# A four-layer Mamba stack and an FP4 FFN on one core: main loop written out, input normalisation and weight quantisation moved into the Mamba prologue, TensorE's side work laid anew on the 16 slots of a turn

## The chip, the core and the metric

One Trainium2 chip, one of its cores. The metric is the device time of one execution in microseconds (us), median of several runs. Engines: PE (TensorE, matmuls), DVE (VectorE), ACT (ScalarE), POOL (GpSimd) and SP (SyncE, which here only issues DMAs).

## What is computed

With `x` of 4 x 2048 x 256 in fp32 (8192 tokens, model width 256, inner width 512, 16 states, convolution of 4 taps, rank 16):

```
x = x + mamba_stack(layernorm(x));  x = x + fp4_ffn(layernorm(x))
mamba_stack, 4 layers:
  xs, z = split(x @ in_w.T);  xc = silu(conv4(xs) + conv_b)
  dt, B, C = split(xc @ xp_w.T);  delta = softplus(dt @ dt_w.T + dt_b)
  h[t] = exp(delta[t] * A) * h[t-1] + delta[t] * xc[t] * B[t]     (512 channels x 16 states)
  y = (sum over states of h * C + xc * D_skip) * silu(z) @ out_w.T
  x = layernorm(y + x) * ln_w + ln_b
fp4_ffn:  q = blockwise FP4 quantise and dequantise, blocks of 16
  down(q(silu(q(x) @ q(wg).T) * (q(x) @ q(wu).T))) with q(wd)
```

## The kernel before, in words

Three blocks of code run one after the other, and the engines meet between them. `normalise_input` brings the 16 chunks of 512 tokens through SBUF two at a time, normalises them on DVE and ACT and writes them to the DRAM buffer `xbuf`. `mamba_layers` runs 64 turns (4 layers x 16 chunks). `fp4_ffn` first quantises and transposes its weights (three pieces of `wgu`, two of `wd`), then runs 16 chunks.

A turn `g` of `mamba_layers` has 16 slots `s`, one for each (32 channels x 4) x (4 states) group: four tiles of 128 rows x 512 tokens. In program order, each engine does in slot `s`:

- DVE: `scan(s,0)`, in slots 2, 6, 10, 14 a `gate` (multiplies the summed states `acc` by `silu(z)`), `times_b(s,1)`, `scan(s,1)`, `scan(s,2)`, `times_b(s+1,0)`, `scan(s,3)`. `times_b` is L935 (`bu<-durep,B_all`, half a slot's tiles), `scan` is L950. LayerNorm statistics of the turn before come in slot 8, their moments in slot 9.
- PE: `broadcast_b(s+1)` (L455, fills the single PSUM tile `B_all`; it waits for `times_b(s,1)`, which reads the old one), then `sum_states(s-2)` (L473, sums `hc` into `acc`), then the slot's side work for the next chunks: `convolve` (L503) in slots 0, 13, 14, 15, `project_x` (L510) in 2, `project_dt` in 3 and 4, `project_out` (L531) in 5 and 6, `project_in` of z in 8 and 9 (L493), `transpose_x` (L483) in 10, `project_in` of xs in 11 and 12. The skip term (L462) opens a quarter of four slots: it comes before `sum_states` in slots 2, 6, 10, 14. All of these but the first two share two PSUM tiles, `W[0]` and `W[1]`, which ACT must have read before PE fills them again.
- ACT: `keep_states(s-1)` (L612, waits for the last scan of the slot before), `exp(s+1)` (L603, 4 tiles), then the copies out of `W`: `copy_z` (L706) of z0, z1 in slot 9 and z2, z3 in 10, `root_guess` and `copy_xT` in 11, `copy_xs` in 12 and 13, `normalise` in 14.
- POOL: `times_c(s)` (L832, `hc<-h,crep`, two instructions), and whole-chunk work: `silu_xc` (L837) ahead of `times_c(2)`, `softplus` steps in slots 7, 8, 10, 11, `variance` (L858) in 10, `affine` (L879 and L883) at the end of slot 15. `project_x` on PE waits for `silu_xc`.
- SP: all loads and stores in one order; `x_res` has one buffer, so `store_x` waits for `affine`, and the next `load_res` for that store.

The first two and the last two turns are written out (`turns`); the 60 between are a loop of 15 iterations of four turns, with register arithmetic for counts and addresses. Nothing but this hand-written order and the semaphores sets what runs when.

Of the kernel before, what the change touches and what calls it, by code (L numbers as in the profile page):

```python
# [5 lines left out]
F32 = mybir.dt.float32  # L6
# [5 lines left out]
P = 128  # L12
T = 512
# [6 lines left out]

LN2 = 0.6931471805599453
# [32 lines left out]
def normalise_input(nc, x, xbuf, CH, sem, x_stored):  # L54

    xv = x.rearrange("(c t p) d -> c p t d", t=NT, p=P)
    ov = xbuf.rearrange("(c t p) d -> c p t d", t=NT, p=P)
    D = x.shape[1]
    with ExitStack() as ctx:
        def sb(name, shape):  # L60
            return ctx.enter_context(nc.sbuf_tensor(name, shape, F32))

        xt = sb("n0_x", [P, 2, NT, D])
        st = sb("n0_stats", [P, NT, 6])
        mean, diff = sb("n0_mean", [P, 2, NT]), sb("n0_diff", [P, NT])
        ve, lnv, guess = sb("n0_var", [P, 2, NT]), sb("n0_ln", [P, 2, NT]), sb("n0_guess", [P, 2, NT])
        tmp, root = sb("n0_tmp", [P, NT]), sb("n0_root", [P, NT])
        loaded = [sem("n0_loaded0"), sem("n0_loaded1")]
        stats, means, var_ready, ln_done, guess_ready = (sem("n0_" + s) for s in ("stats", "means", "var", "ln", "guess"))
        newton, root_done, normed = sem("n0_newton"), sem("n0_root"), sem("n0_normed")  # L70
        block = ctx.enter_context(nc.Block())

        @block.sync
        def _(sp):
            sp.dma_start(xt[:, 0], xv[0]).then_inc(loaded[0], 16)
            sp.dma_start(xt[:, 1], xv[1]).then_inc(loaded[1], 16)
            with sp.Fori(0, CH // 2) as i:
                for b in range(2):
                    sp.wait_ge(normed, 2 * i + b + 1)
                    sp.dma_start(ov[2 * i + b], xt[:, b]).then_inc(x_stored, 16)  # L80
                    sp.wait_ge(x_stored, 16 * (2 * i + b) + 16)

                    sp.dma_start(xt[:, b], xv[(2 * i + 2 + b) % CH]).then_inc(loaded[b], 16)
            for b in range(2):
                sp.wait_ge(loaded[b], 16 * (CH // 2 + 1))

        @block.scalar
        def _(act):
            act.preload_act_table_set(EXP_LN)
            with act.Fori(0, CH // 2) as i:  # L90
                for b in range(2):
                    act.wait_ge(var_ready, 2 * i + b + 1)
                    act.activation(lnv[:, b], ve[:, b], ACT.Ln).then_inc(ln_done, 1)
                    act.wait_ge(ln_done, 2 * i + b + 1)
                    act.activation(guess[:, b], lnv[:, b], ACT.Exp, scale=-0.5).then_inc(guess_ready, 1)

        @block.vector
        def _(dve):
            with dve.Fori(0, CH // 2) as i:
                for b in range(2):  # L100
                    c = 2 * i + b
                    dve.wait_ge(loaded[b], 16 * i + 16)
                    for t in range(NT):
                        dve.bn_stats(st[:, t], xt[:, b, t]).then_inc(stats, 1)
                    dve.wait_ge(stats, NT * c + NT)
                    mean_variance(dve, means, 6 * c, st, D, mean[:, b], diff[:], ve[:, b], var_ready)
                    dve.wait_ge(guess_ready, c + 1)
                    newton_root(dve, newton, 3 * c, ve[:, b], guess[:, b], tmp[:], root[:], root_done)
                    dve.wait_ge(root_done, c + 1)
                    for t in range(NT):  # L110
                        ins = dve.tensor_scalar(xt[:, b, t], xt[:, b, t], mean[:, b, t:t + 1], root[:, t:t + 1],
                                                ALU.subtract, ALU.mult)
                    ins.then_inc(normed, 1)


def mamba_layers(nc, xbuf, w, NL, L, sem, x_stored):
# [13 lines left out]
    assert KD == 2 and DB == 4 and CS == 4 and TOT % 4 == 0 and TOT >= 12 and CH % 4 == 0 and CH >= 4  # L130

    xv = xbuf.rearrange("(c t p) d -> c p t d", t=NT, p=P)

    with ExitStack() as ctx:
# [37 lines left out]
        hc = sb("hc", [P, 8, T])  # L172
        carry = sb("carry", [P, NA])
# [32 lines left out]
        set_up = sem("set_up")  # L206
# [78 lines left out]
        def _(sp):  # L285
# [5 lines left out]
            def load_x(n):  # L291
                c = ready(n % CH)
                if positive(n):
                    sp.wait_ge(w_filled[1], fill(1, n - 1, "tr") + 1)
                if isinstance(n, int):
                    sp.wait_ge(x_stored, 16 * (min(n, CH) + 1))
                sp.dma_start(x_in[:], xv[c]).then_inc(x_loaded, 16)
# [1389 lines left out]
```

## Time and profile before

| what | value |
|---|---|
| median of 3 runs (lowest, highest) | 8526.1 us (8520.08, 8530.0) |
| profiled execution, own time | 8524.19 us |
| its span, first to last instruction | 8522.4 us |
| busy, DVE / POOL / PE / ACT | 93% / 82% / 76% / 63% |
| mean granted clock of TensorE | 0.90 |

A row of the page or of a view names the line, the engine, the operation and the tiles (written `<-` read), a count `x`, and times. "Idle before" is the time the engine stood still just before these instructions, and the arrow names what ended it. A window view gives, for each stretch, each engine's busy time and the granted clock of TensorE as a share of full speed.

### The profile page before, as it was taken

Reading aid. Unit: us, or ns where it says so; the run is one execution under the profiler, and the core shown is the slowest. Engines: PE = TensorE matmul, PEld = TensorE weight load, DVE = VectorE, ACT = ScalarE, POOL = GpSimd, SP = SyncE. Lnnn points to the kernel's source line nnn. Section 1 sums busy time; section 2 is a strip of 40 time slices with the busy share of each in tenths; the row PEclk is TensorE's granted clock in tenths of the full one; section 3 lists DMA queues with packets and bytes.
Section 4 is the critical chain, followed back from the end, with each engine's and each line's share of the span. In section 5 each row is a group of like instructions: output and inputs, shape, how many; then the busy total and the mean of one; then the engine's idle time right before and its main releaser. Section 6 shows DMA issues by size and latency. Waiting matters only on the chain. (4 is left out here: it accounts for less than half of the span.)

```text
span 8522.4 us, 96647 instructions
## 1 busy us (share of the span) xinstructions
PE 6497.0 (76%) x21028; PEld 2513.0 (29%) x21028; DVE 7936.9 (93%) x8028; ACT 5407.2 (63%) x8725; POOL 6990.0 (82%) x3390
## 2 busy tenths in 40 slices
PE   3778777777777777877778777777777777764888
PEld 1222222222222222222222222222222222221555
DVE  3999999999999999999999999999999999995777
ACT  2666666666676666667666666666666666752444
POOL 1888888888888898888888888988888888884555
PEclk9899998988998899889899898989898988986999
DMA  4455443445444544445444454544554444541110
GB/s 134 98 117 120 116 115 97 114 119 132 112 104 111 121 115 113 107 117 123 118 114 112 101 118 115 121 117 107 117 119 117 112 106 106 124 112 43 37 38 30
DMA packets 567641, 909.46 MB, mean 107 GB/s; under 512 B 58288, under 2 KB 202032, under 8 KB 565936
## 3 DMA queue, kind: packets, MB, share of 16 engines
q1 hardware_dynamic: 566960, 902.24, 44.1%
q8 instruction: 201, 3.29, 0.2%
q14 instruction: 480, 3.93, 0.2%
HBM read 715.36 MB, written 186.65 MB: 106 GB/s over the span
## 5 line engine op out<-in xcount | busy, mean ns | idle before, releaser
L832 POOL TENSOR_TENSOR hc<-h,crep 128x1024 f32<-128x1024 f32 x2048 | 4785.2, 2361 | 837.0 <-PE acc L473 755.7
L950 DVE TENSOR_TENSOR_SCAN h<-dA,carry,bu 128x512 f32<-128x512 f32 x3072 | 3769.8, 1266 | 94.3 <-issue 51.8
L935 DVE TENSOR_TENSOR bu<-durep,B_all 128x1024 f32<-128x1024 f32 x2048 | 2485.6, 1214 | 192.1 <-DMA durep<-du_dram 142.5
L603 ACT ACTIVATE dA<-drep,cur 128x512 f32<-128x512 f32 x4096 | 2618.7, 710 | 13.9 <-DMA drep<-delta_dram 13.8
L455 PE MATMUL B_all<-dtc,spread_b 128*128 128x512 f32 x2048 | 1352.2, 747 | 1646.5 <-DVE bu L935 1645.0
L612 ACT COPY carry<-h 128x4 f32<-128x4 f32 x1023 | 201.0, 197 | 2232.2 <-DVE h L950 2184.8
L473 PE MATMUL acc<-hc,gather 128*32 128x512 f32 x8192 | 1279.9, 701 | 4.4 <-POOL hc L832 4.4
L950 DVE TENSOR_TENSOR_SCAN h<-dA,bu 128x512 f32<-128x512 f32 x1024 | 1197.0, 1206 | 9.0 <-ACT dA L603 8.9
L493 PE MATMUL work<-xT,inw 128*128 128x512 f32 x2048 | 1020.2, 643 | 59.5 <-ACT xT L623 48.9
L455 PEld LDWEIGHTS B_all<-dtc,spread_b 128*128 128x128 f32 x2048 | 366.8, 212 | 2330.2 <-DVE bu L935 2266.2
L503 PE MATMUL work<-xs,taps 128*128 128x512 f32 x2048 | 965.2, 614 | 0.0
L493 PEld LDWEIGHTS work<-xT,inw 128*128 128x128 f32 x2048 | 400.6, 207 | 756.1 <-issue 652.1
L503 PEld LDWEIGHTS work<-xs,taps 128*128 128x128 f32 x2048 | 376.6, 194 | 617.6 <-issue 617.6
L531 PE MATMUL work<-outw,sz 128*128 128x256 f32 x2048 | 490.5, 383 | 0.0
L473 PEld LDWEIGHTS acc<-hc,gather 128*32 128x32 f32 x8192 | 173.0, 116 | 972.3 <-issue 686.1
L844 POOL TENSOR_TENSOR quad<-quad,xs 128x2048 f32<-128x2048 f32 x64 | 289.4, 4523 | 154.2 <-ACT quad L701 154.2
L531 PEld LDWEIGHTS work<-outw,sz 128*128 128x128 f32 x2048 | 395.6, 193 | 55.9
L837 POOL TENSOR_TENSOR xc<-xc,quad 128x2048 f32<-128x2048 f32 x64 | 290.0, 4531 | 144.8 <-ACT quad L668 144.8
L1258 PE MATMUL f_gu<-f_wguT,f_xqT 128*128 128x512 f32 (+1 forms) x768 | 341.7, 598 | 72.8 <-ACT f_xqT L1345 65.9
L462 PE MATMUL acc<-xc,skip 128*128 128x512 f32 x512 | 337.6, 749 | 0.0
L854 POOL TENSOR_TENSOR relu<-za,xc 128x2048 f32<-128x2048 f32 x64 | 290.5, 4539 | 0.1
L850 POOL TENSOR_TENSOR za<-quad,relu 128x2048 f32<-128x2048 f32 x64 | 290.0, 4531 | 0.1
(166 smaller groups left out, 6683.6 us busy)
## 6 DMA issues: line engine op xcount, KB each, us to landing
drep<-delta_dram SPq DMA_DIRECT2D x1024, 256.0 KB, 6.0
durep<-du_dram SPq DMA_DIRECT2D x1024, 256.0 KB, 6.7
crep<-c_dram SPq DMA_DIRECT2D x1024, 64.0 KB, 6.4
delta_dram<-za SPq DMA_DIRECT2D x64, 1024.0 KB, 4.3
du_dram<-relu SPq DMA_DIRECT2D x64, 1024.0 KB, 5.3
x_in<-xbuf SPq DMA_DIRECT2D x65, 512.0 KB, 3.9
x_res<-xbuf SPq DMA_DIRECT2D x64, 512.0 KB, 3.9
xbuf<-x_res SPq DMA_DIRECT2D x64, 512.0 KB, 5.6
```

The lines of the kernel that those rows point to most:

```text
L455: pe.matmul(B_all[:], spread_b[:, s % QS, :], dtc[:, p_, :], start=True, stop=True).then_inc(bb_ready, 1)
L462: pe.matmul(acc[:], skip[:, q, :], xc[:, p_, q, :], start=True, stop=False, skip_group_check=True)
L473: ins = pe.matmul(acc[32 * k:32 * k + 32, :], gather[:], hc[:, 4 * (s % 2) + k, :], start=False, stop=s % QS == QS - 1, skip_group_check=True)
L493: ins = pe.matmul(W[b][:], inw[:, k, z * DI + e * P:z * DI + (e + 1) * P], xT[:, k, :], start=k == 0, stop=k == KD - 1)
L503: ins = pe.matmul(W[b][:], taps[:, 4 * e + k, :], xs[:, e, k:k + T], start=k == 0, stop=k == 3)
L531: ins = pe.matmul(half, sz[:, p_, k, t * P:(t + 1) * P], outw[:, k, :], start=False, stop=k == DB - 1)
L603: act.activation(dA[:, 4 * (s % 2) + k, :], drep[q % 2][:, k, :], ACT.Exp, scale=cur[:, p_, 4 * s + k:4 * s + k + 1]).then_inc(da_ready, 1)
L832: pool.tensor_tensor(hc[:, pair, :], h[:, pair, :], crep[:, j:j + 1, :].to_broadcast([P, 2, T]), ALU.mult).then_inc(hc_ready, 1)
L854: pool.tensor_tensor(relu[:], za[:], xc[:, p_], ALU.mult).then_inc(du_ready, 1)
L935: dve.tensor_tensor(bu[:, 2 * k:2 * k + 2, :], durep[q % 2][:, 2 * k:2 * k + 2, :], B_all[:].unsqueeze(1).to_broadcast([P, 2, T]), ALU.mul ...
L950: dve.tensor_tensor_scan(h[:, r, :], dA[:, r, :], bu[:, k, :], start, ALU.mult, ALU.add).then_inc(scanned, 1)
L1258: ins = pe.matmul(gu[:, at:at + width], xqT[:, t % 2, k, :], wguT[:, k, at:at + width], start=k == 0, stop=k == KD - 1)
```

## The change

- `normalise_input` is gone. The 16 raw chunks are loaded, at the start of `mamba_layers`, into tiles that the turns use later (`h`, `hc`, `dA`, `durep`), in batches of 1, 3, 4, 4, 4 chunks; DVE and ACT normalise a batch at a time while PE, ACT and POOL already work on chunk 0.
- The FFN's weights are quantised on DVE and transposed in the same prologue (`quantise_piece`, `turn_piece`, `copy_piece`), saved to DRAM, and only loaded at the start of `fp4_ffn`.
- `turns` writes out all 64 turns; every count and address is then a constant.
- PE: `project_out` works by 128 tokens, one in slots 5 and 6, two in 7; z0, z1 in slot 8, z2 in 9, z3 in 10, ahead of the transposes; the skip term follows `sum_states` of the group's member 1, 0, 0 or 2 (`SKIP_AT`), and the first `sum_states` of a quarter starts the accumulation. The taps of `convolve` run newest first.
- ACT: `copy_out` in slots 7 and 8, `copy_z` of z2 in 10 and z3 in 11, `root_guess` in 12, `normalise` in 15.
- POOL: `variance` in 11, `newton_step` in 13, `affine` after `times_c(0)` of the next turn. DVE: statistics in 9, moments in 10.

```diff
@@ turns
-            turn(0, 0)
-            turn(1, 1)
-            with eng.Fori(0, (TOT - 4) // 4) as i:
-                for r in range(2, 6):
-                    turn(4 * i + r, r % 4)
-            turn(TOT - 2, 2)
-            turn(TOT - 1, 3)
+            for g in range(TOT):
+                turn(g, g % 4)
@@ prologue, sync
+            load_raw(0)
             (the five constants)
             load_inw(0, 0)
+            load_raw(1)
             load_mid(0)
+            load_raw(2)
             load_skip(0, 0)
+            load_raw(3)
+            load_raw(4)
+            store_normed(0)
+            store_normed(1)
+            sp.wait_ge(n0_stored[0], 16)
+            sp.wait_ge(n0_stored[1], 48)
             load_x(1)
+            for i in range(3):
+                load_piece(i)
+            store_normed(2)
             store_c(0, 0)
...
+            for i in range(3, PIECES):
+                load_piece(i)
             store_delta(0, 0)
...
+            sp.wait_ge(piece_copied, PIECES)
+            sp.dma_start(wguT_dram, wguT).then_inc(weights_saved, 16)
@@ sum_states
-                if s % QS == 0:
-                    skip_term(n, p_, s // QS)
+                q = s // QS
+                if s % QS == 0 and positive(DB * n + q):
+                    pe.wait_ge(acc_read, DB * n + q)
...
+                if s % QS == SKIP_AT[q]:
+                    skip_term(n, p_, q)
@@ prologue, tensor
+            turn_piece(0)
             transpose_x(1)
+            turn_piece(1)
             for e in range(DB):
                 project_in(1, e, 0)
+            turn_piece(2)
@@ turn, tensor
-                        if s in (5, 6):
+                        if s in (5, 6, 7):
                             project_out(g - 1, other, s - 5)
+                        if s == 7:
+                            project_out(g - 1, other, 3)
                     if not is_last(g):
-                        if s in (8, 9):
-                            project_in(nxt, 2 * (s - 8), 1)
-                            project_in(nxt, 2 * (s - 8) + 1, 1)
+                        if s == 8:
+                            project_in(nxt, 0, 1)
+                            project_in(nxt, 1, 1)
+                        if s in (9, 10):
+                            project_in(nxt, s - 7, 1)
@@ turn, scalar
-                        if s in (9, 10):
-                            copy_z(n, other, 2 * (s - 9))
-                            copy_z(n, other, 2 * (s - 9) + 1)
+                        if s == 9:
+                            copy_z(n, other, 0)
+                            copy_z(n, other, 1)
+                        if s == 10:
+                            copy_z(n, other, 2)
+                        if s == 11:
+                            copy_z(n, other, 3)
-                        if s == 11:
+                        if s == 12:
                             root_guess(g - 1)
@@ turn, gpsimd
+            pool.wait_ge(weights_saved, 48)
-                        if s == 10:
+                        if s == 11:
                             variance(g - 1)
-                    if not is_first(g):
-                        if s == 15:
-                            affine(g - 1, 0)
-                            affine(g - 1, 1)
+                    if s == 0 and isinstance(g, int) and g >= 2:
+                        affine(g - 2, 0)
+                        affine(g - 2, 1)
@@ prologue, vector: quantise_piece (waits and increments between the steps left out)
+                dve.tensor_reduce(fp_max[:, 0:nb], blocks, AX_X, ALU.max, apply_absolute_value=True)
+                dve.tensor_scalar(fp_scale[:, 0:nb], fp_max[:, 0:nb], 1.0 / 6.0, 1e-12, ALU.mult, ALU.max)
+                dve.tensor_scalar(fp_nudged[:, 0:nb], fp_scale[:, 0:nb], 1.0 + 2.0 ** -21, None, ALU.mult)
+                dve.reciprocal(fp_rec[:, 0:nb], fp_nudged[:, 0:nb])
+                dve.tensor_tensor(blocks, blocks, spread(fp_rec), ALU.mult)
+                dve.tensor_scalar(ex.bitcast(U32), v.bitcast(U32), 0x7F800000, None, ALU.bitwise_and)
+                dve.tensor_scalar(ex, ex, 1.0, MAGIC, ALU.max, ALU.mult)
+                dve.tensor_tensor(v, v, ex, ALU.add)
+                dve.tensor_tensor(v, v, ex, ALU.subtract)
+                dve.tensor_tensor(blocks, blocks, spread(fp_scale), ALU.mult)
@@ prologue, vector
+            n0_statistics(0)
+            n0_normalise(0)
             work_out_a()
+            n0_statistics(1)
+            for i in range(2, len(BATCHES)):
+                n0_statistics(i)
+                n0_normalise(i - 1)
+            n0_normalise(len(BATCHES) - 1)
+            for i in range(PIECES):
+                quantise_piece(i)
             times_b(group(0, 0), 0)
+            dve.wait_ge(piece_turned, PIECES)
+            dve.wait_ge(piece_copied, PIECES)
@@ fp4_ffn, sync
-            sp.dma_start(wgu_in[:].rearrange("p g (t d) -> p (g t) d", d=D),
-                         w["wgu"].rearrange("t p d -> p t d")).then_inc(S["wgu_loaded"], 16)
-            sp.dma_start(wd_in[:], w["wd"].rearrange("(t p) i -> p t i", p=P)).then_inc(S["wd_loaded"], 16)
             load(0, 0)
+            sp.dma_start(wguT[:], wguT_dram).then_inc(S["wgu_loaded"], 16)
+            sp.dma_start(wdT[:, 0:GT - 1], wdT_dram[:, 0:GT - 1]).then_inc(S["wd_loaded"], 16)
```

In `fp4_ffn` the loops over the weight pieces on PE, ACT, POOL and DVE are gone and the counts shifted by as much.

## Rows read from the trace of the kernel before

**Rows 1.** The page's first part: busy time, share of the span, instructions of each engine.

```profile
PE 6497.0 (76%) x21028; PEld 2513.0 (29%) x21028; DVE 7936.9 (93%) x8028; ACT 5407.2 (63%) x8725; POOL 6990.0 (82%) x3390
```

**Rows 2.** Window view, the 64 turns (first scan to end of last): busy times, granted clock.

```profile
216.00:7744.20 7528.20, 5825.52 (x18754) 2126.89 (x18754) 7334.60 (x6902) 5026.88 (x8062) 6560.23 (x2990) 0.90 0.48 113
```

**Rows 3.** Waits of DVE in the turns: us in total, times, longest us.

```profile
DVE h L950 <- issue: 51.8, 8, 6.7
DVE bu L935 <- PE B_all L455: 46.2, 78, 1.3
DVE h L950 <- ACT dA L603: 44.6, 21, 6.5
DVE bu L935 <- DMA durep<-du_dram: 40.8, 35, 2.3
```

**Rows 4.** Groups of instructions, DVE in the turns: busy, mean ns, idle before, its releasers.

```profile
L950 DVE TENSOR_TENSOR_SCAN h<-dA,carry,bu 128x512 f32<-128x512 f32 x3072 | 3769.8, 1266 | 94.3 <-issue 51.8 <-ACT dA L603 35.8 <-POOL hc L832 6.7
...
L950 DVE TENSOR_TENSOR_SCAN h<-dA,bu 128x512 f32<-128x512 f32 x1024 | 1197.0, 1206 | 9.0 <-ACT dA L603 8.9
```

**Rows 5.** Timeline of DVE: first scan of turn 6; start, length, idle before.

```profile
919.16 1.28 DVE L950 TENSOR_TENSOR_SCAN h<-dA,carry,bu 128x512 f32<-128x512 f32 x1 [6.25 <-issue]
```

**Rows 6.** Timeline of DVE and PE ahead of the turns.

```profile
4.41 1.41 DVE L104 BATCH_NORM_STATS2 n_stats<-n_x 128x6 f32<-128x256 f32 x4 [4.41 <-DMA n_x<-in_x]
8.01 1.38 DVE L111 TENSOR_SCALAR n_x<-n_x,n_mean,n_root 128x256 f32<-128x256 f32 x4
...
112.89 1.94 PE L483 MATMUL work<-ident,x_in 128*128 128x128 f32 x8 [112.89 <-DMA x_in<-xbuf]
...
214.69 1.23 DVE L935 TENSOR_TENSOR bu<-durep,B_all 128x1024 f32<-128x1024 f32 x1 [101.69 <-DMA durep<-du_dram]
```

**Rows 7.** Timeline of DVE and POOL at the start of the FFN.

```profile
7793.29 1.22 DVE L1061 TENSOR_REDUCE f_f_qa_amax<-f_wgu_in 128x64 f32<-128x1024 f32 x1 [7.05 <-DMA f_wgu_in<-in_wgu]
...
7840.27 2.35 POOL L1417 TENSOR_TENSOR f_xa<-f_xa,f_xm 128x1024 f32<-128x1024 f32 x1
```

**Rows 8.** Timeline of POOL at the head of turn 20, which starts at 2567.5.

```profile
2570.05 2.36 POOL L879 TENSOR_TENSOR x_res<-x_res,lnw 128x1024 f32<-128x1024 f32 x1
...
2574.79 9.32 POOL L832 TENSOR_TENSOR hc<-h,crep 128x1024 f32<-128x1024 f32 x4
...
2584.08 4.52 POOL L837 TENSOR_TENSOR xc<-xc,quad 128x2048 f32<-128x2048 f32 x1
```

**Rows 9.** Timeline of POOL at the head of turn 1 (no affine), which starts at 329.7.

```profile
334.42 4.76 POOL L832 TENSOR_TENSOR hc<-h,crep 128x1024 f32<-128x1024 f32 x2 [1.75 <-DVE h L950]
341.37 4.75 POOL L832 TENSOR_TENSOR hc<-h,crep 128x1024 f32<-128x1024 f32 x2 [2.19 <-DVE h L950]
```

**Rows 10.** Timeline of PE and DVE in slots 2 and 3 of turn 20.

```profile
2583.87 2.08 PE L455 MATMUL B_all<-dtc,spread_b 128*128 128x512 f32 x2 [5.18 <-DVE bu L935]
...
2589.25 3.70 PE L510 MATMUL work<-xc,xpw 128*128 128x512 f32 x8
...
2592.79 1.02 PE L455 MATMUL B_all<-dtc,spread_b 128*128 128x512 f32 x2
...
2593.94 1.23 DVE L935 TENSOR_TENSOR bu<-durep,B_all 128x1024 f32<-128x1024 f32 x1 [1.05 <-PE B_all L455]
```

**Rows 11.** Window view, PE's work between the two in slot 2: the last columns are clock and DMA.

```profile
2583.90:2589.20 5.30, 5.30 (x12) 1.35 (x12) 5.27 (x5) 5.27 (x10) 4.70 (x2) 0.52 0.01 3
```

**Rows 12.** DMA issues of the page: out<-in, count, KB each, median us to landing.

```profile
xbuf<-x_res SPq DMA_DIRECT2D x64, 512.0 KB, 5.6
```

**Rows 13.** Timeline of all engines in slots 10 and 11 of turn 31 (slot 11 starts at 3945.2).

```profile
3945.26 1.09 PE L483 MATMUL work<-ident,x_in 128*128 128x128 f32 x8
...
3945.43 2.56 ACT L603 ACTIVATE dA<-drep,cur 128x512 f32<-128x512 f32 x4
...
3947.65 1.12 PE L455 MATMUL B_all<-dtc,spread_b 128*128 128x512 f32 x2 [1.29 <-DVE bu L935]
...
3949.86 1.21 DVE L935 TENSOR_TENSOR bu<-durep,B_all 128x1024 f32<-128x1024 f32 x1
```

More of the change, by code:

```diff
@@ L19 @@
 SIGMOID = "sigmoid_and_others"
+MAGIC = 1.5 * 2.0 ** 22
+EXP_CENTRE = -(1.0 - 3e-6)
 LN2 = 0.6931471805599453
@@ L51, in mean_variance @@
     dve.tensor_tensor(ve, ve, diff, ALU.add).then_inc(done, 1)
[L54 to L113, printed above, removed]
@@ L129, in mamba_layers @@
     C_DB, C_CB = 0, DB
-    assert KD == 2 and DB == 4 and CS == 4 and TOT % 4 == 0 and TOT >= 12 and CH % 4 == 0 and CH >= 4
+    SKIP_AT = (1, 0, 0, 2)
     xv = xbuf.rearrange("(c t p) d -> c p t d", t=NT, p=P)
+    raw = x.rearrange("(c t p) d -> c p t d", t=NT, p=P)
+    GP, IN = w["wgu"].shape[0] // NT, w["wd"].shape[1]
+    GT, PIECES = -(-IN // P), GP + w["wd"].shape[0] // P
+    assert KD == 2 and DB == 4 and CS == 4 and TOT % 4 == 0 and TOT >= 12 and CH == 16 and PIECES <= 5 and KD * GP * T <= 8 * T and GT * D <= DB * T
+    BATCHES = [(0, 1), (1, 4)] + [(c, c + 4) for c in range(4, CH, 4)]
     with ExitStack() as ctx:
@@ L501, in convolve @@
                 wait_free(pe, b, fill(b, n, f"c{e}"))
-                for k in range(4):
-                    ins = pe.matmul(W[b][:], taps[:, 4 * e + k, :], xs[:, e, k:k + T], start=k == 0, stop=k == 3)
+                for k in (3, 2, 1, 0):
+                    ins = pe.matmul(W[b][:], taps[:, 4 * e + k, :], xs[:, e, k:k + T], start=k == 3, stop=k == 0)
                 ins.then_inc(w_filled[b], 1)
@@ L525, in project_out, with turn_piece @@
                     pe.wait_ge(res_loaded, 16 * (m + 1))
[L526 to L532 removed]
+                if t % 2 == 0:
+                    wait_free(pe, j, out_fill(j, m))
+                half = W[j][:, (t % 2) * D:(t % 2 + 1) * D]
+                pe.matmul(half, ident[:], x_res[:, t, :], start=True, stop=False)
+                for k in range(DB):
+                    ins = pe.matmul(half, sz[:, p_, k, t * P:(t + 1) * P], outw[:, k, :], start=False, stop=k == DB - 1)
+                if t % 2 == 1:
+                    ins.then_inc(w_filled[j], 1)
+            def turn_piece(i):
+                pe.wait_ge(piece_ready, i + 1)
+                if i > 0:
+                    pe.wait_ge(piece_copied, i)
+                if i < GP:
+                    for k in range(KD):
+                        for t in range(NT):
+                            ins = pe.transpose(bu[:, 2 + k, t * P:(t + 1) * P],
+                                               piece[i % 3][:, t * D + k * P:t * D + (k + 1) * P], ident[:])
+                else:
+                    for k in range(GT):
+                        rows = min(P, IN - k * P)
+                        ins = pe.transpose(bu[0:rows, 2 + k // 4, (k % 4) * P:(k % 4 + 1) * P],
+                                           piece[i % 3][:, k * P:k * P + rows], ident[:])
+                ins.then_inc(piece_turned, 1)
             pe.wait_ge(consts, 80)
@@ L550, in _ @@
             broadcast_b(group(0, 0), 0)
+            for i in range(3, PIECES):
+                turn_piece(i)
             def turn(g, ph):
@@ L584, in _ @@
                 sum_states(group(TOT - 1, s), 1)
-            for j in range(2):
-                project_out(TOT - 1, 1, j)
+            for t in range(NT):
+                project_out(TOT - 1, 1, t)
         @block.scalar
@@ L737, in _ @@
             keep_halo(0)
+            n0_guess_root(1)
             for e in range(DB):
                 copy_conv(0, 0, e)
+            n0_guess_root(2)
             tanh_xc(0, 0)
             act.preload_act_table_set(EXP_LN)
+            for i in range(3, len(BATCHES)):
+                n0_guess_root(i)
             copy_proj(0, 0)
@@ L753, in _ @@
             keep_halo(1)
+            copy_piece(2)
             for e in range(2):
                 copy_conv(1, 1, e)
+            act.wait_ge(n0_stored[3], 64)
             exp(group(0, 0), 0)
+            for i in range(3, PIECES):
+                copy_piece(i)
             def turn(g, ph):
@@ L1011, in turn @@
                     times_b(nxt, 0)
-                    if s == 9 and not is_first(g):
+                    if s == 10 and not is_first(g):
                         dve.wait_ge(stats, g)
@@ L1109, in fp4_ffn @@
     KD = D // P
-    GP = w["wgu"].shape[0] // NT
-    DP, IN = w["wd"].shape[0] // P, w["wd"].shape[1]
+    IN = w["wd"].shape[1]
     GT = -(-IN // P)
```

305 lines of the change are left out of this document (184 added, 121 removed).

## The prediction

> **What bounds the kernel now.** I read the page's busy shares first: DVE is at 93%, well above POOL and PE [rows 1]. Then the window of the 64 turns: DVE is busy 7334.6 of 7528.2 us there [rows 2], 97%. So the turns are DVE's own work plus about 194 us in which it waits; a change in another engine's order counts only through what it adds to or takes from these waits. DVE's waits say which they are [rows 3]: 51.8 us with nothing shown, 44.6 for `exp`, 46.2 for `B_all` from PE, 40.8 for the replicated `du`. The first is eight waits of up to 6.7 us, each ahead of the first scan of a turn, as in turn 6 [rows 5]; six of the waits on `exp` are as long and stand in the same place (the group of carried scans has 35.8 us of them [rows 4]). That is 51.8 + 35.8 = 87.6 us in 14 waits of 6.3 on average, and the loop of 15 iterations jumps back 14 times. What is left to PE and DMA is small and spread. Outside the turns lie 216 us before the first scan and the FFN after.
>
> **The change, part by part.** The sum is made against the profiled execution: span 8522.4 us, own time 8524.2, 1.9 below the median of the runs, 8526.1.
>
> *Prologue.* Before, the first batch is normalised from 4.41 to 9.4 [rows 6], but chunk 0 reaches PE only at 112.89 and the first `times_b` runs at 214.69: a chain of 101.8 us after 112.9 us that are all input normalisation and the start of the block. After, chunk 0 goes to PE straight from the normalised tile at about 13 us (my estimate: the 9.4, and then the steps that work out `A`, for which ACT waits). The chain itself stays: 13 + 101.8 = 115, so 99.7 us are saved if nothing delays it. What DVE adds beside it: 16 chunks at 1.41 + 1.38, 45 us, and five times the 2.2 us of small steps between the two, 11; five pieces of six full-width steps of up to 1.22 us [rows 7] and four small ones, about 9 us for each of the three wide ones and 6.5 for the two narrow ones, 40. 4.4 + 45 + 11 + 40 and 4 for `A` make 104, under 115 if the loads keep up. PE's `turn_piece(1)` and `(2)` stand ahead of chunk 1's convolution, and SP's `load_piece(4)`, ahead of `store_delta`, waits for piece 1 to be turned; a few us late on DVE go straight into the chain. POOL then waits until the weights are saved, a few us that its lead over DVE's second slot mostly covers. I take 90 saved, with 75 and 99 as the ends.
>
> *FFN start.* POOL's first addition, at 7840.27, moves to where the first load lands, about when DVE now gets its first weights, 7793 less 1 us [rows 7]: 48 us saved. The load of the finished weights lies beside the normalising and quantising of chunk 0.
>
> *Loop written out.* The 14 waits of 6.3 us go: 88 saved. The turns 0 to 5 run without one, with the same instructions in a row, so straight code is fed in time, and nothing in the trace speaks against that. The ends are 0 and 88. The Trainium skill (Runtime: NRT & Kernel Launch, Instruction fetch mechanics) says that a taken branch whose target is out of the fetched window stalls the engine and that kernels therefore prefer full unrolling; by it too these 88 us go, and the trace has the 6.25 us it does not state.
>
> *Skip term after the sum, `copy_out` later.* POOL's `times_c` waits for PE's sum; with the skip's two matmuls, of a broadcast's shape (1.02 or 2.08 us [rows 10]), behind the sum, POOL reaches `softplus` and `du` earlier. Of the 40.8 us of `du` waits, and the small ones on `exp` (44.6 - 35.8 = 8.8), I take 33 as saved; 0 and 50 are the ends. The PE rearrangement also evens out slots 5 to 7, so that the 46.2 us of `B_all` waits, taken as a whole, are struck out and new ones counted from nothing below.
>
> *`affine` after `times_c(0)`: the wait in slot 3.* `project_x` waits for `silu_xc`, and PE runs `broadcast_b(4)` behind it, which DVE needs between its third and fourth scan of slot 3. In turn 20 POOL runs `affine` at once after `times_c(15)`, from 2.55 us into the turn, then both `times_c`, and `silu_xc` from 16.58 to 21.1 [rows 8]. POOL would otherwise idle there: without `affine`, `times_c(0)` can't start before 4.72 and ends at 9.48, as in turn 1 [rows 9], because it waits for PE's sum and for the scans. With the new order: 9.48, `affine` 4.78, `times_c(1)` 4.68, `silu_xc` 4.52 make 23.5, which is 2.4 us later. From the start of `project_x` (3.70 us) over the broadcast (1.02) to `times_b(4,0)` it takes 4.69 us, and I give `project_x` 0.15 to start [rows 10]: 28.3. DVE on its own would be there at 25.4 (turn 20 starts a sequence: 2593.94 less its wait of 1.05 and less 2567.5), and in the other turns 12 carried scans of 0.06 us more later [rows 4], at 26.1. POOL, paced by DVE's shorter slots in turns like 20, ends at 23.2 there. So the wait is 2.2 us, and 0.45 more in turns that start a sequence. That is the floor.
>
> On top comes the clock. PE idled 5.18 us before the broadcast in slot 2, which then took 2.08 us where the later one took 1.02 [rows 10], and in the 5.3 us that follow the granted clock is 0.52, the lower level of 1.2 GHz mostly [rows 11]; broadcast, skip and sum fill that stretch, and `project_x` starts at the full clock. After the change the skip is gone from slot 2: the broadcast starts at 16.4 into the turn as now, it and the sum, both at the low clock, end at about 20.4, PE stands about 3.2 us until 23.6, and `project_x` comes out of the pause. I put half of the chain of 4.72 us at the lower level, 2.4 us more; the ends are 0 and 4.7. The Trainium skill (TensorE: Matmul & The Clock Gate, The HAM clock gate) says the array's default state is throttled and that activity releases it; it speaks for the extra, and without it the sum would be 61 x 2.4 = 146 us lower. So 61 turns at 2.2 + 2.4, and 0.45 more in 15 of them: 288 us added. Everything later in the turn shifts along with DVE, so none is won back. On SP `store_x` waits for the later `affine` (its end moves from 7.3 to 14.3 us into the turn), and `load_res`, `load_delta` and `load_du` queue behind it: 14.3 + 5.6 for the store [rows 12] and as much again at most for the load is 25.5 us, before `project_out` in slot 5 at 35, and the `load_delta` behind it waits for slot 3's `exp` in any case. No cost.
>
> *z3 in slot 10: the wait in slot 11.* `transpose_x` fills `W[1]`, which holds z3 until ACT has copied it, and ACT now does so in slot 11 after `exp`: 3945.43 + 2.56, and 0.6 for the copy, make 3948.6. Half the transposes (0.55) and the broadcast (1.12 and 0.13) follow: 3950.4, against 3949.86 on DVE [rows 13]. The floor is 0.55 us. Slot 9 now has one projection in place of two (eight matmuls like those of `project_x`, 3.70 us), so PE's pause before slot 10 grows by 1.85 us, and skip, z3 and transposes run partly at the low clock; I take 1.0 us for 62 turns, 62 us (34 to 124). `root_guess` now stands ahead of `copy_xs` in slot 12 and waits for a `variance` that POOL does behind `times_c(11)`; `project_in` of xs2 waits behind that with no room to spare: 20 us (0 to 60).
>
> Sum: -90 - 48 - 88 - 33 - 46 + 288 + 62 + 20 = +65. 8524.2 + 65 = 8589 us.
>
> **The rivals.** *The clock is no part of it.* PE's work in slot 2 raises the clock as now and the pause is too short to lower it. For it: `project_x` runs at full clock now in turn 20. Against: it does so only because 5.3 us of work precede it. It would give floors only, 288 - 146 + 34 + 10: 8589 - 146 - 28 - 10 = 8405, faster. This is the case on the other side: it is decided by whether `project_x` takes nearer 3.7 or 7.4 us, and the sign changes where the clock costs 1.3 us a turn instead of 2.4.
>
> *No wait in slot 3 at all.* `silu_xc` isn't what PE is late for, because POOL makes up the 2.4 us. Against: between `times_c(1)` and `silu_xc` nothing in its order leaves room. 8405 - 142 = 8263.
>
> *The long waits stay.* The written-out code is fetched no faster, or the 14 waits are not the jump's. Against: their place and number. 8589 + 88 = 8677.
>
> *The whole chain at the low clock.* 4.7 instead of 2.4 us in 61 turns: 8589 + 140 = 8729, more if slot 11 goes the same way.
>
> **How the numbers follow.** Forecast 0.44 (its own range 8500 to 8660), no clock 0.30, no wait in slot 3 0.07, waits stay 0.06, whole chain low 0.13. The range runs from 8385, which holds the first rival with 20 us to spare, to 8700, which holds the third and leaves out the second and most of the last. A difference under 0.2% (17 us) can't be told from none. Faster by more: the 0.37 of the two lower cases and 0.03 of the forecast, 0.40; within: 0.12, where the clock's share comes out near 1.3 us; slower: 0.48.
>
> **What would show it.** After: no wait of 6 us before a first scan; first scan between 117 and 130 us; the FFN's first addition some 8 us into its block; `B_all` waits of DVE up from 46 us to over 300, most between 2 and 6 us and in slot 3, a second set near 1 us in slot 11; `project_x` over 3.7 us in most turns; PE's granted clock lower in slot 3. The prediction is wrong if the `B_all` waits stay below 150 us, or the long waits remain.

## The result and the profile after

| what | before | after |
|---|---|---|
| median (lowest, highest), 5 runs each | 8524.36 us (8514.69, 8530.0) | 8570.91 us (8569.6, 8571.52) |
| span of the profiled execution | 8522.4 us | 8569.5 us |
| mean granted clock | 0.90 | 0.90 |

The ratio is 1.0056, 95% interval 1.0041 to 1.0071: slower by 0.56%. The forecast was 8589 us.

The page's busy shares of the changed kernel, as [rows 1]:

```profile
PE 6538.7 (76%) x21028; PEld 2499.6 (29%) x21028; DVE 7941.4 (93%) x7922; ACT 5385.8 (63%) x8693; POOL 6973.0 (81%) x3380
```

Its window view, the 64 turns (first scan to end of last), as [rows 2]: length, then busy us of PE, weight load, DVE, ACT and POOL, clock, DMA share, GB/s.

```profile
134.30:7835.30 7701.00, 5868.72 (x18758) 2114.22 (x18758) 7325.41 (x6902) 5018.20 (x8062) 6562.01 (x2990) 0.90 0.47 110
```

Its waits of DVE from 100 to 7830 us, as [rows 3]: us in total, times, longest.

```profile
DVE bu L1007 <- PE B_all L456: 363.2, 138, 5.9
DVE bu L1007 <- DMA durep<-du_dram: 16.6, 13, 8.0
DVE h L1022 <- ACT dA L636: 1.6, 1, 1.6
```

Its groups, as [rows 4]: busy, mean ns, idle before with releasers. The last two are PE's.

```profile
L1022 DVE TENSOR_TENSOR_SCAN h<-dA,carry,bu 128x512 f32<-128x512 f32 x3072 | 3760.4, 1263 | 0.0
...
L499 PE MATMUL work<-xT,inw 128*128 128x512 f32 x2048 | 1039.8, 649 | 176.4 <-ACT xs L673 158.8
...
L516 PE MATMUL work<-xc,xpw 128*128 128x512 f32 x512 | 365.5, 879 | 181.0 <-POOL xc L907 181.0
```

The first scan comes at 134.3 instead of 216.0: 81.7 us won. The turns take 7701.0 instead of 7528.2: 172.8 lost. From the end of the turns to the end of the last `affine` it is 37.6 instead of 38.4. POOL's first addition of the FFN comes 9.4 us after that instead of 57.7: 48.3 won. The rest of the FFN is 5 us longer; DVE's waits ahead of `f_hid` are as much longer there (42.3 instead of 37.1 us), and the cause is open. Together +47, the difference of the spans.

In the turns DVE's own work is 9.2 us less and its idle time 182 more. The rows split it: the waits of 6 us ahead of a first scan are gone (87.6 in [rows 3, 4]); `du` keeps 8.6 of 40.8 (16.6 less the first, which lies ahead of the turns); the small ones on `exp` keep 1.6 of 8.8; `B_all` goes from 46.2 to 363.2, +317. By slot, when each of the 138 is laid on its turn in the timeline: 258.6 us in slot 3, 87.4 in slot 13, 16.7 in slot 11.

**Slots 2 and 3 of turn 20**, which starts at 2537.2; all engines, as [rows 8, 10]: start, length, idle before.

```profile
2542.76 4.66 POOL L902 TENSOR_TENSOR hc<-h,crep 128x1024 f32<-128x1024 f32 x2 [3.02 <-PE acc L473]
...
2547.38 2.36 POOL L949 TENSOR_TENSOR x_res<-x_res,lnw 128x1024 f32<-128x1024 f32 x1
...
2552.12 4.68 POOL L902 TENSOR_TENSOR hc<-h,crep 128x1024 f32<-128x1024 f32 x2
...
2553.93 1.80 PE L456 MATMUL B_all<-dtc,spread_b 128*128 128x512 f32 x2 [4.28 <-DVE bu L1007]
...
2556.77 4.51 POOL L907 TENSOR_TENSOR xc<-xc,quad 128x2048 f32<-128x2048 f32 x1
...
2561.34 5.25 PE L516 MATMUL work<-xc,xpw 128*128 128x512 f32 x8 [3.74 <-POOL xc L907]
...
2566.42 1.02 PE L456 MATMUL B_all<-dtc,spread_b 128*128 128x512 f32 x2
...
2567.54 1.23 DVE L1007 TENSOR_TENSOR bu<-durep,B_all 128x1024 f32<-128x1024 f32 x1 [4.72 <-PE B_all L456]
```

`times_c(0)` waits 3.02 us for PE's sum, so `affine` stands between it and `times_c(1)`, and `silu_xc` ends at 2561.28, 24.1 us into the turn. `project_x` then takes 5.1 us up to the broadcast, where it took 3.5 in [rows 10], and DVE waits 4.72. The window view of the stretches just before and in it:

```profile
2557.60:2561.30 3.70, 0.00 (x0) 0.00 (x0) 3.70 (x4) 3.70 (x8) 3.70 (x2) 0.96 0.39 101
2561.30:2566.40 5.10, 5.06 (x8) 2.27 (x9) 1.52 (x2) 0.81 (x2) 4.59 (x2) 0.69 1.04 229
```

PE stands for 3.7 us at a granted clock of 0.96, and with it back at work the clock is 0.69, a share of it at the lower of its two levels, 1.2 GHz. Finer windows show that it was at the lower level in most of the broadcast and sum before the pause (0.55 in these 3.7 us), rose when PE had stopped, fell again at 2561.1, just before PE resumed, and was back at 1.00 from 2564.7 on. It read 0.50 from 2561.3 to 2564.4, so about 3.1 of the 5.1 us up to the broadcast ran at the lower level.

Turn 20 starts a sequence. In the turns 17 to 19, which do not, the pause is shorter, 2.5 us. The clock stays at 0.50 through it in turns 17 and 18 and rises in turn 19 (0.92), and in the stretch behind it reads 0.67, 0.54 and 0.67. Turn 17, pause and then most of `project_x`:

```profile
2197.00:2199.50 2.50, 0.00 (x1) 0.00 (x0) 2.50 (x3) 2.27 (x5) 2.50 (x2) 0.50 0.82 265
2199.50:2204.30 4.80, 4.77 (x8) 2.20 (x9) 2.81 (x3) 0.86 (x2) 4.59 (x2) 0.67 1.06 223
```

**Slots 11 to 13 of turn 20**, all engines, as [rows 13]:

```profile
2622.59 0.66 PE L489 MATMUL work<-ident,x_in 128*128 128x128 f32 x4 [0.71 <-ACT sz L739]
...
2623.08 1.02 PE L456 MATMUL B_all<-dtc,spread_b 128*128 128x512 f32 x2
...
2624.20 1.23 DVE L1007 TENSOR_TENSOR bu<-durep,B_all 128x1024 f32<-128x1024 f32 x1
...
2633.26 0.21 POOL L928 TENSOR_TENSOR ve<-mv,c_eps 128x4 f32<-128x4 f32 x1
...
2633.51 0.20 ACT L747 ACTIVATE lnv<-ve 128x4 f32<-128x4 f32 x1 [4.26 <-POOL ve L928]
...
2633.94 1.06 ACT L673 COPY xs<-work 128x512 f32<-128x512 f32 x2
...
2634.57 3.70 PE L499 MATMUL work<-xT,inw 128*128 128x512 f32 x8 [3.62 <-ACT xs L673]
...
2639.17 1.23 DVE L1007 TENSOR_TENSOR bu<-durep,B_all 128x1024 f32<-128x1024 f32 x1 [1.46 <-PE B_all L456]
```

In slot 11 PE waits 0.71 us for z3 and DVE not at all. In slot 12 an instruction on 128 x 4 elements, `variance`, stands on POOL behind `times_c(11)`; ACT waits for it 4.26 us in `root_guess`, with `copy_xs` queued behind it; PE's `project_in` waits 3.62, and the broadcast behind it is late for DVE. Turn 20 is a mild case: of the other turns that start a sequence, 14 have a wait of 4.0 to 4.1 us in slot 13, 56.7 us of the 87.4.

**Prologue**, DVE and POOL (piece 0's first small step, then piece 1):

```profile
71.12 0.20 DVE L1108 TENSOR_SCALAR fp_scale<-fp_max 128x64 f32<-128x64 f32 x1
...
78.55 1.21 DVE L1106 TENSOR_REDUCE fp_max<-h 128x64 f32<-128x1024 f32 x1
79.79 3.77 DVE L1108 TENSOR_SCALAR fp_scale<-fp_max 128x64 f32<-128x64 f32 x1
83.60 4.56 DVE L1110 TENSOR_SCALAR fp_nudged<-fp_scale 128x64 f32<-128x64 f32 x1
88.19 0.55 DVE L1112 RECIPROCAL fp_rec<-fp_nudged 128x64 f32<-128x64 f32 x1
88.78 4.98 DVE L1114 TENSOR_TENSOR h<-h,fp_rec 128x1024 f32<-128x1024 f32 x1
93.79 4.87 DVE L1116 TENSOR_SCALAR h<-h 128x1024 uint32<-128x1024 uint32 x1
...
132.92 1.23 DVE L1007 TENSOR_TENSOR bu<-durep,B_all 128x1024 f32<-128x1024 f32 x1 [8.03 <-DMA durep<-du_dram]
```

```profile
79.00 4.51 POOL L914 TENSOR_TENSOR quad<-quad,xs 128x2048 f32<-128x2048 f32 x1 [30.33 <-ACT quad L734]
...
88.19 4.49 POOL L920 TENSOR_TENSOR za<-quad,relu 128x2048 f32<-128x2048 f32 x1
92.76 5.35 POOL L924 TENSOR_TENSOR relu<-za,xc 128x2048 f32<-128x2048 f32 x1
```

Of DVE's steps of piece 1 four are drawn out, and each ends no more than 1.1 us after one of POOL's four does (the second runs from 83.59 to 88.11): piece 1 takes 24.5 us (78.55 to 103.08) where piece 0 took 8.7 (69.88 to 78.55). SP's queue turns that into delay:

```profile
85.77 19.81 SPq L370 DMA_DIRECT2D h<-in_wd  x2
105.62 0.43 SPq L333 DMA_DIRECT2D delta_dram<-za  x1
```

The second of the two `load_piece` waits until piece 1 is turned; `store_delta` behind it goes out at 105.62, though POOL had `za` ready at 92.68. DVE had been held up once before in the same way: the sixteen `tensor_scalar` that normalise the third batch took 9.43 us (from 42.29), one of them 4.58 instead of 0.40, beside POOL's `silu_xc` (43.94 to 48.67); the last batch's sixteen took 5.26.

### The profile page after: what moved, and what is told of

Same layout as the page of the kernel before. It is cut to its first block and busy times, and to the rows that moved or that the text cites. A ratio compares the mean times of both kernels' runs of the same rounds, so it can differ in the third digit from the quotient of the medians.

```text
span 8569.5 us, 75181 instructions
## 1 busy us (share of the span) xinstructions
PE 6538.7 (76%) x21028; PEld 2499.6 (29%) x21028; DVE 7941.4 (93%) x7922; ACT 5385.8 (63%) x8693; POOL 6973.0 (81%) x3380
## 5 line engine op out<-in xcount | busy, mean ns | idle before, releaser
L1007 DVE TENSOR_TENSOR bu<-durep,B_all 128x1024 f32<-128x1024 f32 x2048 | 2478.2, 1210 | 382.0 <-PE B_all L456 363.2
L456 PE MATMUL B_all<-dtc,spread_b 128*128 128x512 f32 x2048 | 1292.1, 716 | 1459.5 <-DVE bu L1007 1439.5
L473 PE MATMUL acc<-hc,gather 128*32 128x512 f32 x8192 | 1257.8, 689 | 4.4 <-POOL hc L902 4.4
L499 PE MATMUL work<-xT,inw 128*128 128x512 f32 x2048 | 1039.8, 649 | 176.4 <-ACT xs L673 158.8
L456 PEld LDWEIGHTS B_all<-dtc,spread_b 128*128 128x128 f32 x2048 | 343.3, 204 | 2147.2 <-DVE bu L1007 2077.1
L509 PE MATMUL work<-xs,taps 128*128 128x512 f32 x2048 | 942.0, 603 | 0.0
L516 PE MATMUL work<-xc,xpw 128*128 128x512 f32 x512 | 365.5, 879 | 181.0 <-POOL xc L907 181.0
```

Source lines behind the costliest of these rows:

```text
L456: pe.matmul(B_all[:], spread_b[:, s % QS, :], dtc[:, p_, :], start=True, stop=True).then_inc(bb_ready, 1)
L473: ins = pe.matmul(acc[32 * k:32 * k + 32, :], gather[:], hc[:, 4 * (s % 2) + k, :], start=s % QS == 0, stop=s % QS == QS - 1, skip_group_c ...
L499: ins = pe.matmul(W[b][:], inw[:, k, z * DI + e * P:z * DI + (e + 1) * P], xT[:, k, :], start=k == 0, stop=k == KD - 1)
L509: ins = pe.matmul(W[b][:], taps[:, 4 * e + k, :], xs[:, e, k:k + T], start=k == 3, stop=k == 0)
L516: ins = pe.matmul(W[0][:], xpw[:, k, :], xc[:, p_, k, :], start=k == 0, stop=k == DB - 1)
L1007: dve.tensor_tensor(bu[:, 2 * k:2 * k + 2, :], durep[q % 2][:, 2 * k:2 * k + 2, :], B_all[:].unsqueeze(1).to_broadcast([P, 2, T]), ALU.mul ...
```

## The experiments

The kernel before, run beside them, had medians of 8522.0, 8520.2 and 8522.6 us, and 8524.4 beside the changed kernel. Each ratio is to the kernel before as run beside it; differences to the changed kernel are between medians of different sittings, so a few us of them mean nothing.

**affine back in slot 15.**

```diff
-                    if s == 0 and isinstance(g, int) and g >= 2:
-                        affine(g - 2, 0)
-                        affine(g - 2, 1)
+                    if s == 15 and not is_first(g):
+                        affine(g - 1, 0)
+                        affine(g - 1, 1)
...
-            for k in range(2):
-                affine(TOT - 2, k)
```

> The changed kernel with one thing undone: affine stands at the end of slot 15 again, as before. My theory: POOL's affine fills the idle stretch ahead of times_c(0), silu_xc ends 2.4 us earlier in the turn, PE's pause ahead of project_x shrinks to under 1 us and with it the stretch at the low clock. DVE's waits for B_all in slot 3 fall from 259 us to 30 to 70, project_x from 5.7 to about 4 us, the whole from 8571 to about 8360 (8330 to 8400). If it is PE's own new order that makes PE late in slot 3, the time stays within 20 us of 8571. If the order costs but the clock does not follow, about 8430.

Measured: 8374.69 us (8369.43 to 8384.33), ratio to before 0.9826 [0.9809, 0.9842], 196 under the changed kernel. Its waits of DVE, and `project_x`:

```profile
DVE bu L1005 <- PE B_all L456: 183.8, 123, 4.1
```
```profile
L516 PE MATMUL work<-xc,xpw 128*128 128x512 f32 x512 | 289.6, 716 | 39.9 <-POOL xc L907 39.8
```

Slot 3 falls from 258.6 to 50 us of waits, so `affine`'s new place is what PE and then DVE are late by. Slot 13 rises from 87 to 125: with DVE 3 us a turn faster, `variance` comes still later for the copy behind it. A part of the gain is given back there.

**Skip term of quarter 0 one slot earlier**, in slot 2 behind the sum, ahead of PE's pause:

```diff
-    SKIP_AT = (1, 0, 0, 2)
+    SKIP_AT = (0, 0, 0, 2)
```

> The changed kernel with the skip term of the first quarter right after the sum of its first member, so in slot 2 and ahead of project_x, while affine stays late. My theory: the order's 2.2 us a turn stay, and about half or more of the clock's 2 us a turn go, since PE works on through most of the pause: project_x from 5.7 to about 4.3 us, 8571 to about 8470 (8440 to 8500). If the clock has no part in slot 3, nothing changes (8560 to 8580).

Measured: 8450.44 us (8445.85 to 8454.26), 0.9915 [0.9898, 0.9931], 120 under the changed kernel. DVE waits 249.0 us for `B_all`, 137.8 of them in slot 3. `project_x`:

```profile
L516 PE MATMUL work<-xc,xpw 128*128 128x512 f32 x512 | 246.0, 625 | 73.3 <-POOL xc L907 73.3
```

**Dummy work ahead of the wait.** Two matmuls of the program (four records, since each shows as two, like those of `project_x`), whose result `project_x` overwrites, go into its tile while PE would wait for `silu_xc`; nothing else moves.

```diff
@@ project_x
-                pe.wait_ge(xc_ready, n + 1)
                 wait_free(pe, 0, fill(0, n, "xp"))
+                if n >= 2:
+                    for k in range(2):
+                        pe.matmul(W[0][:], xpw[:, k, :], dtc[:, 1 - p_, :], start=True, stop=True)
+                pe.wait_ge(xc_ready, n + 1)
```

> The changed kernel with two idle matmuls of a broadcast's shape added ahead of project_x, into the PSUM tile that project_x then overwrites, before the wait for silu_xc: the same dependences, more PE work, the same order. My theory: the pause is filled, project_x takes about 4 us, DVE's B_all waits in slot 3 fall from 259 to 150 to 190 us, the whole to about 8480 (8450 to 8510). If the clock has no part in it, the added work changes nothing or costs (8565 to 8600).

Measured: 8445.34 us (8441.54 to 8449.39), 0.9909 [0.9893, 0.9926]. More work, 126 us less time, and a little under the range expected:

```profile
DVE bu L1010 <- PE B_all L456: 242.6, 136, 4.1
```
```profile
L519 PE MATMUL work<-xc,xpw 128*128 128x512 f32 x512 | 239.7, 612 | 32.3 <-POOL xc L910 32.1
```

One `project_x` matmul takes 612 ns on average instead of 879, as in the kernel before, 613 (the records of neighbours overlap, so eight of them are no sum). In turn 20 the clock was 0.50 in the broadcast and sum ahead of the dummy work; then, `project_x` and its stretch up to the end of the broadcast:

```profile
2523.29 3.70 PE L519 MATMUL work<-xc,xpw 128*128 128x512 f32 x8 [0.27 <-POOL xc L910]
```
```profile
2523.30:2527.90 4.60, 4.60 (x14) 1.93 (x18) 2.03 (x2) 0.95 (x2) 4.55 (x2) 1.00 1.06 220
```

It is the full clock, as it is for `project_x` of turn 20 in the run with the skip term moved (also 3.70 us). Slot 3 keeps 135.0 us of waits. So the other 123.6 of the 258.6, 2.0 us a turn, are the clock's. That agrees with the Trainium skill (TensorE: Matmul & The Clock Gate, The HAM clock gate): activity is what releases the throttle.

**root_guess behind copy_xs** (in the last two turns, which have no `copy_xs`, at its old place):

```diff
-                        if s == 12:
+                        if s == 12 and isinstance(g, int) and g >= TOT - 2:
                             root_guess(g - 1)
...
                                 copy_xs(g + 2, (ph + 2) % 4, 2 * (s - 12) + 1)
+                                if s == 12 and not is_first(g):
+                                    root_guess(g - 1)
```

> The changed kernel with root_guess behind the copies of xs0 and xs1 in ACT's slot 12, not ahead of them. My theory: the copies no longer wait for POOL's variance, PE's project_in of xs2 starts up to 3.6 us earlier, and DVE's B_all waits in slot 13 fall from 87 us to under 10: 8571 to about 8490 (8480 to 8500). If slot 13 is late because of PE's own work in slots 10 to 12, the 87 us stay and the time is within 10 us of 8571.

Measured: 8510.22 us (8501.38 to 8518.25, 10 runs), 0.9987 [0.9977, 0.9997], 61 under the changed kernel. Its waits of DVE:

```profile
DVE bu L1009 <- PE B_all L456: 275.1, 79, 5.9
DVE bu L1009 <- DMA durep<-du_dram: 43.1, 40, 8.0
DVE h L1024 <- POOL hc L904: 8.9, 15, 0.8
```

Slot 13 has no wait left, so the mechanism is shown. The time is 10 us over the range expected; of the 87.4 us, 26.5 came back as waits for `du` at the end of slot 15 (43.1 less 16.6), and 8.9 as waits for POOL.

**The kernel before with its turns written out**, nothing else of the change:

```diff
@@ turns, of the kernel before
-            turn(0, 0)
-            turn(1, 1)
-            with eng.Fori(0, (TOT - 4) // 4) as i:
-                for r in range(2, 6):
-                    turn(4 * i + r, r % 4)
-            turn(TOT - 2, 2)
-            turn(TOT - 1, 3)
+            for g in range(TOT):
+                turn(g, g % 4)
```

> The kernel before with only its 64 turns written out in place of the loop. My theory: the 14 waits of 6.3 us at the jump back go and little else moves: 8522 to about 8430 (8415 to 8445), with no wait of 6 us ahead of a turn's first scan. If those waits are not the jump's, they stay and the time is within 15 us of 8522.

Measured: 8437.82 us (8430.69 to 8439.96), 0.9905 [0.9888, 0.9921], 82 under before. The carried scans wait for nothing but POOL:

```profile
L945 DVE TENSOR_TENSOR_SCAN h<-dA,carry,bu 128x512 f32<-128x512 f32 x3072 | 3771.8, 1268 | 10.0 <-POOL hc L827 10.0
```

So the long waits belong to the loop. They stood ahead of turns 6, 10, 14 and so on to 58, each the first of an iteration, and not ahead of the turns within one. Whether the jump itself or the loop's own register arithmetic takes the time no run separates.

**DVE kept off POOL's softplus.** It waits ahead of piece 1 until `du` is ready.

```diff
@@ quantise_piece
                 dve.wait_ge(piece_loaded[i], 16)
+                if i == 1:
+                    dve.wait_ge(du_ready, 1)
```

> The changed kernel where DVE, ahead of quantising piece 1 in the prologue, waits until POOL has finished its softplus steps and du. In the changed kernel piece 1 takes 24.6 us beside POOL's work and the others 8.5. My theory: the two engines hinder each other there; with the wait piece 1 takes 8.5 us, starting some 19 us later, POOL's last step takes 4.5 us and not 5.4, and the first scan comes at 138 (134 to 140) us for the 134.3 now: within 6 us of 8571, on either side. If the slow steps of piece 1 had another cause (its load, its data), it would take about 24 us again and the first scan come at about 150: 8587.

Measured: 8573.83 us (8566.77 to 8577.5), 1.0061 [1.0044, 1.0078]. DVE, and POOL's last softplus step:

```profile
98.93 1.22 DVE L1108 TENSOR_REDUCE fp_max<-h 128x64 f32<-128x1024 f32 x1 [18.98 <-POOL relu L924]
...
107.61 1.21 DVE L1108 TENSOR_REDUCE fp_max<-h 128x64 f32<-128x1024 f32 x1
```
```profile
94.34 4.49 POOL L924 TENSOR_TENSOR relu<-za,xc 128x2048 f32<-128x2048 f32 x1
```

Piece 1 takes 8.7 us alone, and POOL's step 4.49 instead of 5.35: the two do hinder each other. Nothing is won, since DVE spends the time waiting: the first scan comes at 139.0, where 138 was expected.

**All three repairs together**: affine in slot 15, `SKIP_AT[0] = 0`, `root_guess` behind `copy_xs` (edits as above).

> The changed kernel with all three mended: affine at the end of slot 15, the first skip term ahead of project_x, root_guess behind copy_xs. Alone they gave 196, 121 and 61 us. The first two overlap (both shorten slot 3's 259 us), and with affine moved slot 13's waits grew from 87 to 125 us, so that the third is worth more. B_all waits under 30 us in all, some 40 to 60 us of du waits back in slot 15: 8571 to about 8265 (8240 to 8300). If the three were no more than what each gave alone at its best, 8193; if slot 13's waits turn into du waits fully, 8310.

Measured: 8295.49 us (8290.51 to 8297.29), 0.9735 [0.9719, 0.9752]: 275 under the changed kernel and 225 under before.

```profile
DVE bu L1007 <- PE B_all L456: 57.8, 82, 1.6
DVE bu L1007 <- DMA durep<-du_dram: 45.5, 42, 7.7
```

Taken singly the three gave 196, 120 and 61, 377 in all. The first two overlap: with `affine` early PE hardly waits for `silu_xc`, so that little is left for a clock to cost. Under 30 us of `B_all` waits were expected and 57.8 are there, 43.2 of them in slot 3, where the kernel before had 28.3, and 11.1 in slot 11.

**And the z projections back in slots 8 and 9, two each**:

```diff
-                        if s == 8:
-                            project_in(nxt, 0, 1)
-                            project_in(nxt, 1, 1)
-                        if s in (9, 10):
-                            project_in(nxt, s - 7, 1)
+                        if s in (8, 9):
+                            project_in(nxt, 2 * (s - 8), 1)
+                            project_in(nxt, 2 * (s - 8) + 1, 1)
...
                         if s == 10:
                             copy_z(n, other, 2)
-                        if s == 11:
                             copy_z(n, other, 3)
```

> As the kernel with all three mended, with z2 and z3 both in PE's slot 9 and copied in ACT's slot 10, as before. My theory: z3's late copy is what makes slot 11 late, by 5 to 20 us in all, and these go: 0 to 15 us faster than with all three mended. If PE needs the spread, it is slower.

Measured: 8294.23 us (8293.74 to 8294.66), 0.9735 [0.9719, 0.9752], the same. The waits in slot 11 go, and others come: all 58.9 us for `B_all` are now in slot 3, and DVE waits 16.2 us for `exp`.

**The three repairs, and load_piece(4) behind store_du:**

```diff
-            for i in range(3, PIECES):
-                load_piece(i)
+            load_piece(3)
             store_delta(0, 0)
             load_delta(0, 0, 0)
             load_delta(0, 0, 1)
             store_du(0, 0)
+            load_piece(4)
```

> The combined version (affine in slot 15, SKIP_AT[0] = 0, root_guess behind copy_xs), and SP's load_piece(4) moved from ahead of store_delta(0,0) to behind store_du(0,0). In the changed kernel POOL's softplus was ready at 92.7 us, but SP issued store_delta only at 105.6, because load_piece(4), ahead of it, waited for piece 1 to be turned (15.8 us late on DVE beside POOL). Theory (the queue holds the chain): store_delta at about 92.7, store_du at about 101, the replicated du for the first times_b at about 119, and DVE, now the later of the two, is through with its pieces at about 125; first scan at about 126 to 127 instead of 134.3, about 8 us less in all: 8287 us. Rival (piece 4 then arrives late, or the transfer of delta is slow for another reason, the loads in flight): DVE waits for piece 4 ahead of its last quantisation or the chain still ends near 133; first scan 131 or later, 8292 to 8297 us.

Measured: 8289.82 us (8288.35 to 8292.79), 0.9726 [0.9713, 0.9739]: the lowest median of all, though the interval overlaps that of the version without this edit. SP and DVE:

```profile
95.64 0.37 SPq L333 DMA_DIRECT2D delta_dram<-za  x1
```
```profile
132.33 1.22 DVE L1022 TENSOR_TENSOR_SCAN h<-dA,bu 128x512 f32<-128x512 f32 x1 [2.17 <-ACT sz L776]
```

`store_delta` no longer waits for the queue (`za` was ready at 95.61), as the theory has it, and DVE, through with its pieces at 127.8, is the later of the two. The first scan was to come at 126 to 127 and came at 132.3, which is where the rival had it (131 or later), though not by the rival's ways: DVE does not wait for piece 4, and the chain of `du` no longer ends last. What held it: POOL's softplus started 2.9 us later in this execution (81.93), piece 1 was drawn out beside it as before, and DVE waited 1.1 us for `B_all` and 2.2 more for ACT's last copy of a piece ahead of the scan. So the queue did hold the chain, but the first scan is 1.5 us earlier than in the version without this edit (133.86), not 8; of the 6 us between the medians that is a part, and the two ranges overlap.

## Why the prediction was right, and where not

The sign, the place and the kind were right: DVE's new waits for `B_all` are what the change costs, most of it in slot 3, and they outweigh a shorter prologue, a shorter start of the FFN and the straight code. The terms, us against the profiled execution of before:

| step | forecast | measured |
|---|---|---|
| prologue | -90 | -81.7 |
| FFN start | -48 | -48.3 |
| loop written out | -88 | -87.6 (alone: -82) |
| `du` and small `exp` waits | -33 | -39.4 |
| old `B_all` waits out | -46 | -46.2 |
| slot 3 | +288 | +258.6 |
| slot 11 | +62 | +16.7 |
| slot 13 | +20 | +87.4 |
| not in the forecast: DVE's own work, other small waits, the FFN's rest | 0 | -9, -8, +4 |
| sum | +65 | +47 |

That the sum comes within 18 us of the measured time is in part luck: slot 13 was 67 us too cheap, slots 3 and 11 29 and 45 too dear, and these errors nearly cancel.

- *Slot 3.* The floor was put at 141 us (2.2 a turn, 0.45 more in 15) and is 135.0, by the run with dummy work. The clock was put at 2.4 us a turn between ends of 0 and 4.7, and is 2.0. That half the chain runs at the low level was a middle between two ends with no row for it; the windows show that kind of stretch (0.69 and 0.67), and the size came near by luck. The path to it was drawn too simply: a pause of about 3.2 us out of which PE comes at the low level. In the turns 17 to 19 it is 2.5 us, and in turn 20 it is 3.7; in 17 and 18 the clock stays at 0.50 through it, in 19 and 20 it rises in it and falls again.
- *Slot 11, mis-sized.* The 1.0 us assumed half a microsecond of low clock in it. In turn 20 PE ran the transposes in 0.49 us up to the broadcast and this in 1.02, both the short forms. The 0.3 us a turn that were measured are less than even the floor without any clock, 0.55, and the second set of waits that was announced for slot 11 stands in slot 13.
- *Slot 13, the step that was too small.* The mechanism stood in the forecast: `root_guess` ahead of `copy_xs`, waiting for a `variance` behind `times_c(11)`, with "no room to spare"; it was given 20 us (0 to 60) without being worked out. In [rows 8] POOL's `times_c` pair takes 4.7 us, and in turns that start a sequence, where DVE's slots are short, it puts the broadcast 4.0 to 4.1 us late in 14 of them (56.7 us); the rest is spread over 26 more turns, at most 1.7 in each. The run without it has none of the 87.4.
- *`du` waits, right for a wrong reason.* They were to shrink because the skip term is out of POOL's way. They shrank because DVE was held in slot 13 first: with this wait gone, 26.5 us of them come back.
- *Old `B_all` waits, right for a wrong reason.* They were struck out because slots 5 to 7 would be evened out. Only 8.9 of the 46.2 us lay there (slots 6 and 7), and 28.3 in slot 3. It comes out even so, because slot 3 was counted anew from DVE's own pace.
- *Prologue, 8 us short.* The first scan was to come between 117 and 130 and came at 134.3. The forecast priced the quantisation by rows of the FFN in which DVE and POOL take turns. The chain up to `za` ran as forecast: 13 + 76.3 (112.89 to 189.22 in the old trace) is 89, against 92.7. From `za` to the first scan it was 26.8 us before; 92.7 + 26.8 = 119.5, and 12.9 us in SP's queue make 132.4, against 134.3. The way was named ("a few us late on DVE go straight into the chain"), the 15.8 us were not, nor the 4.2 lost on the third batch.

Of the rivals, that the clock is no part of it is refuted by the dummy work and by the skip's slot, two ways to the same 120 to 126 us. No wait in slot 3 and the long waits staying are refuted by the trace. The whole chain at the low clock would have needed 7.4 us for `project_x`, whose row in turn 20 is 5.25.

## What to carry to other kernels

A small instruction put ahead of a copy or a matmul that others need must be priced like a large one: by what its own operand waits behind, not by its length (`variance` and `root_guess`, 0.2 us each, cost 87 us of waits). Where PE stops for some microseconds (2.5 to 3.7 here) ahead of work on which the bound engine waits, expect a part of that work at its lower clock (about 3.1 of 5.1 us in turn 20), and look for independent work to put before the pause: moving the skip term, one matmul of the program, by one slot gave 120 us. And take the sum of single gains as an upper end, since waits that are removed come back at the next thing that had been hidden (26.5 of 87 us, and 377 us singly against 275 together).

## What the hardware showed that was not expected

DVE and POOL hinder each other, but only in some instructions. Beside POOL's two-input operations of 4.5 us, DVE's `tensor_scalar` on 64 columns took 3.77 and 4.56 us instead of 0.20, one on 1024 columns 4.87 instead of 0.69, and a `tensor_tensor` with both inputs in SBUF 4.98 instead of 1.23, while a reduction (1.21) and a `reciprocal` (0.55) went through unhindered, as does `times_b` in the turns, whose `B_all` lies in PSUM (1.21 beside POOL at 85%). It goes both ways: POOL's last step took 5.35 instead of 4.49. The trace of the kernel before has one such place too, in the FFN: POOL's step that started at 7823.76 ends at 7825.69, and a `tensor_scalar` of DVE started within it takes 1.29 us (from 7824.44) where its neighbour of the same shape takes 0.19. The Trainium skill (SBUF — State Buffer, SBUF: two separate sides) says that the port pair the two share is locked for the whole instruction by whoever starts first, against VectorE when it runs in a two-port mode or reads two SBUF inputs; the trace agrees in each of these cases. The forecast could have looked for the 15.8 us by it, since its own times put DVE's quantisation beside POOL's softplus.
